# Twenty-nine stages on one core: eleven more of them have their first loads issued by the stage before, and the biased attention copies its output behind the exponentials

## The reference, cut to what matters

```
A: q, k, v = x @ W_qkv + b;  rotary;  16 heads of 16, causal softmax;  x = LN(x + o @ W_proj + b)
B: two layers: local attention (8 heads of 64, window 128), x + o @ wo; LN; a * gelu(g); x + h @ w2;  then LN
C: 16 heads of 16, softmax(q k^T * s + bias[k - q])  (a learned relative bias, not causal);  LN(x + o @ Wo)
D: x and weight quantised in blocks of 32 (6 bits), x_q @ w_q + bias;  LN
E: a linear state-space mixer: project, short convolution, scan over time, project;  LN
   a mixture of 16 routed and 2 shared experts;  LN
G: a linear recurrence over time with complex states (lru);  LN
H: as B, with other weights;  the last LN writes the output
```

## Time and profile before

| what | value |
|---|---|
| device time, median of 3 runs | 7195.08 us (7183.85 to 7199.11) |
| profiled execution, its own time | 7190.16 us |
| its span in the profile | 7188.4 us |
| PE busy | 5935.6 us, 83% of the span |
| DVE busy | 4627.3 us, 64% |
| ACT busy | 2685.7 us, 37% |
| POOL busy | 1335.2 us, 19% |

### The profile page before, as it was taken

One profiled execution on the slowest core, in us unless ns is written; L12 is line 12 of the kernel. 1 busy time (PEld: TensorE's weight loads), 2 busy tenths in 40 slices (PEclk: granted clock), 3 DMA queues, 4 the chain that ended last, 5 costly groups with the idle time before them and its releaser, 6 DMA issues. The chain is left out here.

```text
span 7188.4 us, 109924 instructions
## 1 busy us (share of the span) xinstructions
PE 5935.6 (83%) x31088; PEld 3325.9 (46%) x31088; DVE 4627.3 (64%) x11763; ACT 2685.7 (37%) x6018; POOL 1335.2 (19%) x1059
## 2 busy tenths in 40 slices
PE   5799869989988977888863679977995888998989
PEld 2344334755466542333332443344553456554755
DVE  4666567733864657999968549973335775457736
ACT  0166514712463203666630125531110364224711
POOL 1211116100621021000000005530003531025100
PEclk9899979989999987999985889988997999999989
DMA  4333255662456434233322221133222457235641
GB/s 144 92 78 77 61 154 154 198 201 76 147 181 198 130 112 112 77 92 81 86 80 71 83 74 37 37 89 106 67 55 84 138 174 228 65 96 157 190 156 56
DMA packets 914667, 807.21 MB, mean 112 GB/s; under 512 B 241832, under 2 KB 770176, under 8 KB 913920
## 3 DMA queue, kind: packets, MB, share of 16 engines
q1 hardware_dynamic: 502128, 507.31, 24.4%
q10 hardware_dynamic: 389888, 274.83, 12.3%
q0 software_dynamic: 22144, 18.99, 0.8%
HBM read 506.25 MB, written 316.67 MB: 114 GB/s over the span
## 5 line engine op out<-in xcount | busy, mean ns | idle before, releaser
L1567 ACT ACTIVATE Catt_E<-Catt_t 128x512 f32<-128x512 f32 x1024 | 565.4, 595 | 307.8 <-DVE Catt_t L1530 257.4
L1516 DVE CUSTOM_DVE_ANT_0 Catt_S<-Catt_s,Catt_win 128x1024 f32<-128x1024 f32 x512 | 621.1, 1215 | 12.2 <-DMA Catt_win<-skewed 10.6
L1516 DVE CUSTOM_DVE_ANT_0 Aatt_S<-Aatt_s,Aatt_win 128x128 f32<-128x128 f32 (+7 forms) x512 | 373.2, 756 | 187.9 <-PE Aatt_s L1437 184.1
L1567 ACT ACTIVATE Aatt_E<-Aatt_t 128x512 f32<-128x512 f32 (+3 forms) x768 | 335.1, 492 | 215.7 <-PE Aatt_t L1469 136.2
L1466 PE MATMUL Catt_t<-Catt_Q,Catt_K 123*128 123x512 bf16 x1024 | 328.4, 382 | 100.8 <-ACT Catt_E L1567 72.5
L1437 PE MATMUL Catt_s<-Catt_K,Catt_Q 96*128 96x512 bf16 x1024 | 320.8, 396 | 49.3 <-DVE Catt_nmax L1516 29.4
L1530 DVE TENSOR_TENSOR Catt_t<-Catt_t,Catt_near 128x256 f32<-128x256 f32 (+2 forms) x640 | 281.1, 456 | 73.9 <-PE Catt_t L1466 66.4
L2550 PE MATMUL scan_cum<-scan_X,scan_upto 128*128 128x512 f32 x512 | 265.4, 608 | 26.7 <-DVE scan_X L2619 25.0
L1488 PE MATMUL Catt_o<-Catt_E,Catt_V 128*32 128x256 f32 x4096 | 273.9, 385 | 0.0
L2548 PE MATMUL scan_cum<-scan_X,scan_after 128*128 128x512 f32 x448 | 239.6, 617 | 39.8 <-DVE scan_pi L2630 39.8
L1437 PE MATMUL Aatt_s<-Aatt_K,Aatt_Q 96*128 96x512 bf16 (+3 forms) x768 | 217.9, 340 | 39.7 <-DVE Aatt_nmax L1516 24.1
(11 more groups left out here) (778 smaller groups left out, 14094.4 us busy)
## 6 DMA issues: line engine op xcount, KB each, us to landing
area<-oT_s SPq DMA_DIRECT2D x16, 1024.0 KB, 6.5
area<-rows SPq DMA_DIRECT2D x256, 64.0 KB, 2.0
moe_cb<-c_s SPq DMA_DIRECT2D x16, 1024.0 KB
skewed<-lines POOLq DMA_DIRECT2D x8, 1920.0 KB, 12.8
Catt_win<-skewed SPq DMA_DIRECT2D x16, 960.0 KB, 4.8
rec<-state_in_r ACTq DMA_DIRECT2D x32, 416.0 KB
scan_r<-rec SPq DMA_DIRECT2D x64, 208.0 KB, 2.4
Catt_near<-near_s SPq DMA_DIRECT2D x32, 384.0 KB
```

What stands on the lines that cost most here:

```text
L1516: v.tensor_tensor_reduce(out=S[:, j % 2, 0:w], in0=s_ps[j % 2][:, 0:w], in1=win[:, 0 if causal else h, w0:w0 + w], scale=-1.0, scalar=BIG, ...
L1567: a.activation(E[:, kb % NB, h, lo:hi], bank(it, n)[:, 0:hi - lo], ACT.Exp, scale=scale).then_inc(exped, 1)
```

## The change

Eleven more stages get a front: Aqkv, Aatt, Aout, Cqkv, Catt, Cout, Dmx, state_in, scan, moe and lru. Only enter and Eout stay without. The new classes have the same two methods; two of them in full, with the loads of the others below in words:

```diff
+class ThinFront(Front):
+
+    def __init__(self, nc, area, name, q_s, k_s, v_s, bias=None):
+        super().__init__(area)
+        self.open(nc, name)
+        self.q_s, self.k_s, self.v_s, self.bias = q_s, k_s, v_s, bias
+        k1 = TERMS * 16 + PARTS + (PARTS * NT if bias else 0)
+        self.Q, self.K = (self.area[0:k1, self.words(T)].bitcast(BF16).rearrange("p (h t) -> p h t", h=2) for _ in range(2))
+        self.V = self.sb(NT * 2, 32).rearrange("p (k h) d -> p k h d", h=2)
+        self.head_in, self.late_in = self.sem("head_in0"), self.sem("late_in0")
+        if bias:
+            self.near = self.sb(2, 3 * P)
+
+    def words(self, n):
+        self.used += n
+        return slice(self.used - n, self.used)
+
+    def weights(self, sp):
+        self.issued = True
+        if self.bias:
+            windows, nears, ext = self.bias
+            sp.dma_start(self.K[TERMS * 16 + PARTS:], ext[0:2 * PARTS * NT, :].rearrange("(h p) c -> p h c", h=2)).then_inc(self.late_in, 16)
+            sp.dma_start(self.near, nears[0:2 * P, :].rearrange("(h p) c -> p h c", h=2)).then_inc(self.late_in, 16)
+
+    def inputs(self, sp):
+        heads = lambda x: x[0:2 * PARTS * 16, 0:T].rearrange("(h p) c -> h p c", h=2)
+        for t0, nt, part in STACK:
+            rows = slice(t0 * 16, (t0 + nt) * 16)
+            sp.dma_start(self.Q[rows], heads(self.q_s)[:, 0:nt * 16].rearrange("h p c -> p h c")).then_inc(self.head_in, 16)
+            for h in range(2):
+                sp.dma_start(self.K[rows, h], heads(self.k_s)[h:h + 1, part * 16:(part + 1) * 16].to_broadcast([nt, 16, T])
+                             ).then_inc(self.head_in, 16)
+        for h in range(2):
+            sp.dma_start(self.V[:, :, h, 0:16], self.v_s[0:T, h * 16:(h + 1) * 16].rearrange("(t p) d -> p t d", p=P)).then_inc(self.late_in, 16)
...
+class ScanFront(Front):
+
+    def __init__(self, nc, area, name, rec, theta, width):
+        super().__init__(area)
+        self.open(nc, name)
+        self.rec, self.theta, self.width = rec, theta, width
+        self.th, self.r = self.sb(theta.shape[-1]), self.sb(8, width)
+        self.th_in, self.r_in = self.sem("th_in"), [self.sem(f"r_in{i}") for i in range(8)]
+
+    def weights(self, sp):
+        self.issued = True
+        sp.dma_start(self.th, self.theta.partition_broadcast(P)).then_inc(self.th_in, 16)
+
+    def inputs(self, sp):
+        for j in range(8):
+            sp.dma_start(self.r[:, j, :], self.rec[j * P:(j + 1) * P, 0:self.width]).then_inc(self.r_in[j], 16)
+
```

Stages of B and H change as well. `LocalOutFront` now holds both chunks, and the order on SP is another; DVE does the ffn's first norm in the out stage:

```diff
             front.issue(sp)
-            load(0, 1)
             with sp.Fori(1, B - 1) as it:
                 for c in range(2):
                     load(it, c)
-            load(B - 1, 0)
-            ahead.weights(sp)
-            load(B - 1, 1)
             sp.wait_ge(z_out[0], 16 + 16)
             ahead.inputs(sp)
+            for c in range(2):
+                load(B - 1, c)
+            ahead.weights(sp)
...
@@ -1201,6 +1416,8 @@
                         v.wait_ge(z_out[c], it * 16 + 16)
                     v.wait_ge(y_done, it * NT + (u + 1))
                     v.tensor_tensor(z[:, c, q, :], y[q][:], rs[c][:, q, :], ALU.add).then_inc(z_done, 1)
+                    if it == B - 1 and u == 3:
+                        ahead.norm(v)
```

In the thin attentions Q, K, V and near become one tile for each batch, K's and V's ones are written in four pieces (V's only in the columns that keep them), and:

```diff
+                    for b in range(B):
+                        sp.dma_start(Q[b][r:r + NT], of[:].unsqueeze(1).to_broadcast([NT, 2, T])).then_inc(put, 16)
...
             def load(it, b):
+                if b == 0 and isinstance(it, int):
+                    front.issue(sp)
+                    if not causal:
+                        window(it, 0)
+                    return
                 if b == 1 and not causal and not isinstance(it, int):
                     window(it, 0)
...
-                if b == 0 and not causal and isinstance(it, int):
-                    window(it, 0)
-                if b == 0 and isinstance(it, int):
+                if b == 1 and isinstance(it, int):
                     sp.wait_ge(V_ones, 1)
...
             pipelined(sp, PAIRS, B, ((3, maxima), (0, load)))
+            ahead.weights(sp)
+            sp.wait_ge(o_out[0], 64 + 64 * PAIRS)
+            ahead.inputs(sp)
...
-            written_out(t, PAIRS, ST, ((0, scores), (TURN, turn_maxima), (LAG, scores_by_key), (LAG + 3, values_of_block)))
+            written_out(t, PAIRS, ST, ((0, scores), (TURN, turn_maxima), (LAG, scores_by_key), (LAG + 3, values_of_block if causal else values)))
...
-            copy, exps = (LAG + 4, move_out), (LAG, exp)
-            written_out(a, PAIRS, ST, ((TURN, move_maxima), *((exps, copy) if causal else (copy, exps)), (LAG + 11, write_sums),
+            written_out(a, PAIRS, ST, ((TURN, move_maxima), (LAG, exp), (LAG + 4, move_out), (LAG + 11, write_sums),
                                      (LAG + 15, spread_sums), (LAG + 23, store)))
```

More of the change, by code:

```diff
@@ L537, in spread, with stage_enter @@
         g.wait_ge(out, 32 * len(pairs))
-def stage_enter(nc, x, act0, acts, tables, logs, bias):
+def stage_enter(nc, x, act0, acts, tables, logs, bias, ahead):
     with ExitStack() as ctx:
@@ L657, in _ @@
                     tail.load(sp, it, u)
+            ahead.weights(sp)
+            tail.first_columns(sp)
+            ahead.inputs(sp)
         @block.gpsimd
@@ L3191, in bass_post_layernorm_stack @@
+    stage_enter(nc, i["L0_attn_x"], a0, acts, tables, i["L3_logs"], bias, ahead=thin)
+    heads = ThinFront(nc, areas[0], "Aatt", q_parts, k_parts, v_s)
+    stage_qkv(nc, "Aqkv", thin, a0, q_parts, k_parts, v_s, 1.0, ahead=heads)
+    joint = ThinOutFront(nc, areas[1], "Aout", oT_s, i["L0_attn_W_proj"], a0)
+    stage_thin_attention(nc, "Aatt", heads, q_parts, k_parts, v_s, nm_s, r_s, oT_s, 0.25, ahead=joint)
     front = first_front("B", "L0_ffn", a1)
-    stage_thin_out(nc, "Aout", oT_s, i["L0_attn_W_proj"], a1, a0, bias=i["L0_attn_b_proj"], ahead=front)
@@ new lines, in bass_post_layernorm_stack @@
+    joint = ThinOutFront(nc, areas[0], "Cout", oT_s, i["L1_wo"], cur)
+    stage_thin_attention(nc, "Catt", heads, q_parts, k_parts, v_s, nm_s, r_s, oT_s, 0.25, ahead=joint, bias=tables_b)
+    quant = MxFront(nc, areas[1], "Dmx", nxt, i["L1_ffn_weight"])
+    stage_thin_out(nc, "Cout", joint, oT_s, nxt, cur, ahead=quant, cols=False)
+    cur, nxt = nxt, cur
+    state = StateFront(nc, areas[0], "state_in", nxt, i["L2_attn_W_in"], i["L2_conv"], i["L2_attn_score_scale"], i["L2_slopes"],
+                       i["L2_mix"], i["L2_dist"])
@@ new lines, in bass_post_layernorm_stack @@
+    stage_mx_project(nc, "Dmx", quant, cur, nxt, cur, i["L1_ffn_bias"], ahead=state)
+    cur, nxt = nxt, cur
+    rec = scratch("rec", [B * T, 2 * REC])
+    scan = ScanFront(nc, areas[1], "scan", rec, i["L2_theta"], REC)
+    stage_state_inputs(nc, state, cur, rec, ahead=scan)
+    stage_state_scan(nc, scan, rec, o_s)
+    experts = ExpertsFront(nc, areas[0], "moe", nxt, i["L2_ffn_router_w"], i["L2_wg"], i["L2_wu"])
+    stage_project(nc, "Eout", o_s, C, i["L2_attn_W_out"], nxt, cur, act=ACT.Silu, ahead=experts)
```

546 lines of the change are left out of this document (336 added, 210 removed).

## The result

The changed kernel takes 7125.55 us in the median of four runs (7120.85 to 7132.27), the kernel before 7195.78 us beside it. The ratio is 0.9906, with a 95% interval of 0.9889 to 0.9923: 70 us less, where 65 were forecast. The profiled execution has a span of 7120.1 us, 68.3 us less than before.

The account below looks back on a forecast made before the run. PE, busy some five sixths of the span, mostly bounds the kernel, with DVE setting Catt's pace. Fronts -71, local out stages -39 and reorder +45 make -65 us: 7195.1 to 7130 us, range 7070 to 7178.

Parts of the forecast that it names:

- the fronts: Starts of stages: first loads issued in the stage before remove waits, 71 us less in all.
- the out stages: Four local out stages with the ffn starts behind them: 9.8 us less each, 39 us in all.
- The reorder of Catt: Biased attention's batch changes: values in halves and copy behind the exponentials cost 45 us, between +25 and +64.
- The stall: Catt's batch change: DVE stands 1.8 to 1.9 us; net +0.8 us a change, 2.05 with a clock fall.
- rival B: Catt: the reorder wins, up to 34 us; 7050, or 7085 with Catt breaking even; chance 0.20.
- the scan: Start of the scan stage: DVE's idle time of 9.52 us falls to 5.17, 4.4 us less.
- Aout's term: Start of Aout: residuals loaded ahead let DVE start near 915.2 instead of 919.28, 4 us less.
- The gaps to the ffn: Start of the ffn: PE's 10.39 us wait for the norm becomes 5.17, 5.2 us less at each of four.
- the norm's overhang: Local out stage: the ffn's layer norm, now on DVE there, sticks out 1.1 us beside PE's work.
- the moved issues: SP issues moved into the stage before lie behind its last loads, where SP stands idle.
- Rival C: Stage tails: half of the fronted time is not won; mostly 7150 to 7180, about 7185 at worst; chance 0.18.
- Rivals D and E: D: Catt's new wait propagates, 7225 at 4.5 us a batch, chance 0.08; E: within 14 us of 7195, chance 0.06.

Follow-up runs that it names:

- E1: The changed kernel with both edits of Catt's order undone (whole blocks of values, copy ahead of the exponentials): 7083.39 us, ratio 0.9844.
- E4: The kernel before with only the two edits of Catt's order (halves, copy behind the exponentials), no new fronts: 7231.93 us, ratio 1.0049.
- E2: The changed kernel with only ScalarE's order in Catt undone (values in halves, copy ahead of the exponentials): 7056.94 us, ratio 0.9808.
- E5: E2 with the first layer norm back at the ffn's own start: 7067.50 us, ratio 0.9821.
- E6: E2 with the local attention issuing the next stage's weights and residuals later, at batch 2 of its last pair: 7067.56 us, ratio 0.9819.
- E10: E2 with only the first chunk of the local out stage's input loaded ahead, the second by the stage itself: 7045.44 us, ratio 0.9788.
- E12: E10 with, in addition, K's ones written by GpSimd instead of DVE in both thin attentions: 7050.15 us, ratio 0.9790.

## Why the prediction was right

The total was, 7130 for 7125.55. No term was off by more than 8 us, and the misses partly cancel: the fronts and the rest of the span gave 6 us more than forecast, Catt cost 5 us less, the out stages gave 8 us less. The terms:

- **The reorder of Catt** was forecast at +45 us, the middle of +25 with the clock kept and +64 with it fallen. Measured in 29 of the 31 batch changes: +40.1 us, where the same share of 45 is 42. The stall was walked at 1.8 to 1.9 us and is 1.96 us. PE's wait for the copy is 2.19 us in all 29, but the clock falls in only 18 of them: those batches take 29.6 us or more, with one stretch at a granted clock of 0.50 in each, and the other 11 take 28.3 to 28.4 us, with none (DVE waits of 2.5 us in all). Against the same batches of the kernel before this is +1.96 and +0.44 us. So the forecast of 2.05 us for a batch with a fall was right, and the 0.8 us for one without was 0.36 too high. That the middle of the two came out is in part luck: nothing in the prediction said that three changes in five would have a fall. E1 and E4 show the cost alone, 42 and 37 us. The Trainium skill (TensorE: Matmul & The Clock Gate, Part 1) says that the half rate is the default and that activity releases it. The falls here fit that. But the sentence names no gap after which the upper level is lost, so the prediction could not get its +64 us from it.
- **What the prediction had not seen** is that the loss was one of the pair. It priced both edits as a whole, rightly, and the gain that it had as its lower bound and in rival B, -34 us, is near what the halves win when the copy stays in front: E2 is 26.5 us below E1, and its batches are 1.16 us shorter. PE's waits for the copy show the pair too: 0.59 us with the halves alone, 0.58 us with the copy behind alone, 2.19 us with both.
- **The fronts** were forecast at 71 us. By the table they are 72 (all rows but Catt's 3rd to 31st batch and the out stages), and 5 us more of the span's 68.3 lie in stages that the table leaves out. The rows came out within 2.1 us of the forecast, but for the scan (7.8 for 4.4). There the boundary was right too: PE's gap went from 25.0 to 20.7 us, which is 4.3, and the other 3.5 lie inside the stage, which took 476.3 to 485.8 us in the builds with the new fronts. In moe likewise the gap gave 9.1 us of the 12.2. Two stages did not run as before: Aqkv gave back 6.2 of 12.1 us, lru won 6.5 more, and other builds with the same loads show either value. Their 384 matmuls each kept PE busy for 162.6 us instead of 156.5 and 114.6 instead of 121.1, with a granted clock of 0.86 against 0.90 and 0.86 against 0.81. Over the eleven experiments with the new fronts Aqkv took 186.2 to 192.7 us and lru 185.5 to 192.4 us with the same code. One slip of the working: 913.48 + 2.0 is 915.5 and not 915.2, so Aout's term was 3.8 us and not 4 (3.9 measured).
- **The local out stages** are the term that was mis-sized: 39 us forecast, 31.2 measured. In four stages together, from PE's first matmul to its last, they gave 24.3 us for the forecast 22.8: the waits for the last chunk went (0.8 us stayed in the first of them). The gaps to the ffn gave 13.9 us for 16.4, with the norm's overhang in both numbers; the norm makes DVE end 1.1 us later, as forecast, and E5 prices it at 14.6 us. What was overlooked is the other end: PE's four gaps between attention and out stage grew from 63.4 to 70.4 us, 7 of the missing 8 us. The prediction said that the moved issues lie behind a stage's last loads, where SP stands idle. In the local attention two chunks instead of one now stand on SP ahead of the last stores. In the nine builds with two chunks and early weights these gaps sum to 70.0 to 73.9 us, and to 83.0 with the weights late (E6); E4, with one chunk as before, has 66.2, E10 63.0 and E12 66.3.
- **Rival C** (half of the fronted time lost to the tails) did not hold, except for these 7 us. The Trainium skill (DMA: Bandwidth & Descriptors, "Issuing engines are not separate DMA queues") says that all DMAs run on the same 16 engines and interleave. No run here separates that from the order on SP, so which of the two delays the stores is not shown. Rivals D and E did not happen.

What stays open: why the granted clock of Aqkv, lru, moe and scan differs from build to build by some us a stage, and why the same wait of 2.19 us lets the clock fall in one batch change and not in the next. Neither was tried. No run takes out a single front, the split of the tiles by batch or the new order of loads in the out stage; their terms rest on the traces before and after.

## What to carry to other kernels

Walk the batch change, engine by engine, when an order changes: the rows of one change and their durations gave the new stall within 0.2 us. Price two edits that meet at one buffer in all four combinations, since here the halves alone were worth 27 us, the copy's place alone was worth nothing or cost 5 us, and the pair cost 40. A load moved into the stage before can win its whole wait (in moe 9.1 of 15.3 us, down to the 6.2 us of a boundary), but look at the last stores of that stage behind it in the queue; and an order that is right for one form of a stage (the copy first, where DVE sets the pace) may be wrong for its sister (the exponentials first, where PE waits for their banks).

## What was not expected of the hardware

A memset of 3 rows by 8192 took 6.88 us; as four of 3 by 2048 it took 1.76 us each with 0.38 us between them, 8.2 us in all. By these rows the split puts the first mask 1.3 us later; no run has the single memset beside a front, so that price is not shown. And the same 384 matmuls of Aqkv kept PE busy for 156.5 us before and 162.6 us after: the clock fell in seven of eight gaps of 3.6 to 4.0 us before and in all of the same eight after, and stood at its lower level for 36 us in the one build and 53 in the other. Differences of 6 us in one stage say nothing of an edit until they show in several kernels.
